# Stacked queries, keys and maxima by transfers instead of turns, the weights' causal corner by GpSimd, 48-row products on 128 rows, and a new order

## What is computed

```python
# block 0: 16 heads of 16 channels
q = split_heads(x @ Wq + bq); k = split_heads(x @ Wk + bk); v = split_heads(x @ Wv + bv)
attn = jnp.einsum('bhqd,bhkd->bhqk', q, k) / jnp.sqrt(jnp.float32(D))
attn = attn + slopes[:, None, None] * (jnp.arange(T) - (T - 1))[None, None, :]
attn = jnp.where(causal, attn, jnp.finfo(jnp.float32).min)
o = jnp.einsum('bhqk,bhkd->bhqd', jax.nn.softmax(attn, axis=-1), v)
out = o.transpose(0, 2, 1, 3).reshape(B, T, C) @ Wo + bo
# block 3: no mask, rope of the halves t1, t2 of each head of q and k
out = jnp.concatenate([t1 * cos - t2 * sin, t1 * sin + t2 * cos], axis=-1)
```

## Time and profile before

| | us |
|---|---|
| three timed runs | 1338.24, 1340.66, 1344.62 |
| median | 1340.66 |
| span of the profiled execution | 1338.5 |
| TensorE matmul busy | 1212.3 (91%) |
| VectorE busy | 938.6 (70%) |
| ScalarE busy | 666.7 (50%) |
| GpSimd busy | 413.8 (31%) |
| bytes moved by transfers | 52.80 MB |

### The profile page before, as it was taken

The page is one execution under the profiler, slowest core; times in us unless marked ns, Lnnn a source line. Parts: engine busy times, 40 slices in busy tenths (PEclk is TensorE's granted clock), DMA queues, the critical chain, the costliest instruction groups (busy, mean ns, idle before and its releaser), DMA issues.

```text
span 1338.5 us, 19778 instructions
## 1 busy us (share of the span) xinstructions
PE 1212.3 (91%) x7788; PEld 796.3 (59%) x7804; DVE 938.6 (70%) x1779; ACT 666.7 (50%) x976; POOL 413.8 (31%) x394
## 2 busy tenths in 40 slices
PE   1789999999999989897789999998999899799988
PEld 0567777677655554554358888886346346445544
DVE  8978575776658999852766645389778676877671
ACT  5335565654767777552133323131772564375473
POOL 3655540034002242402562214034313411421310
PEclk9989999998999999999599999998899889999989
DMA  7200000000060000173530000004101000100200
GB/s 214 67 1 1 2 1 2 2 1 1 1 235 17 16 32 8 56 222 123 132 53 1 24 1 1 1 20 98 29 1 48 1 1 1 47 1 1 95 1 17
DMA packets 31581, 52.80 MB, mean 39 GB/s; under 512 B 5280, under 2 KB 19712, under 8 KB 30720
## 3 DMA queue, kind: packets, MB, share of 16 engines
q1 hardware_dynamic: 27408, 40.57, 9.4%
q0 software_dynamic: 4080, 10.97, 3.7%
HBM read 43.57 MB, written 10.52 MB: 40 GB/s over the span
## 4 chain that ended last, share of the span: by engine, by line
PE 59%; DVE 24%; ACT 6%; issue 5%; POOL 3%; DMA 3%; SPq 0%; DVEq 0%; ACTq 0%; POOLq 0%
PE pair L648 17%; PE bank L648 16%; PE bank L736 7%; PE pair L724 5%; PE pair L704 5%; DVE max L1146 3%; PE pair L686 3%; ACT probs L1641 2%; PE pair L715 2%; DMA gathered<-outbox,slots 2%; POOL gathered L2010 1%; PE pair L694 1%; DVE xn L1065 1%; DVE hidden L1196 1%; PE bank L744 1%
## 5 line engine op out<-in xcount | busy, mean ns | idle before, releaser
L1146 DVE TENSOR_REDUCE max<-pair 128x2 f32<-128x1024 f32 (+3 forms) x256 | 254.7, 1021 | 110.6 <-PE pair L694 57.1
L1641 ACT ACTIVATE probs<-pair 128x1024 f32<-128x1024 f32 (+3 forms) x256 | 212.7, 868 | 94.0 <-PE pair L694 53.5
L704 PE MATMUL pair<-ks,qs 50*128 50x512 f32 (+3 forms) x512 | 117.2, 472 | 17.8 <-DVE max L1146 6.4
L1968 POOL TENSOR_TENSOR h_low<-hidden,h_high 128x512 fp32r<-128x512 f32 x64 | 83.4, 1310 | 133.8 <-ACT h_high L1681 133.4
L736 PE MATMUL bank<-probs,v 128*32 128x512 f32 (+3 forms) x1024 | 114.2, 529 | 0.7 <-ACT probs L1641 0.7
L724 PE MATMUL pair<-qs,ks 52*128 52x512 f32 (+3 forms) x512 | 107.7, 442 | 7.8 <-DVE max L1146 2.7
L704 PEld LDWEIGHTS pair<-ks,qs 50*128 50x128 f32 x512 | 50.9, 198 | 76.3 <-DVE max L1146 28.7
L2028 POOL TENSOR_TENSOR h<-mix_h,h 128x512 bf16<-128x512 f32 x48 | 56.0, 1180 | 125.3 <-DVE mix_h L1537 72.0
L724 PEld LDWEIGHTS pair<-qs,ks 52*128 52x128 f32 x512 | 47.9, 187 | 77.5 <-ACT probs L1641 22.3
L1673 ACT ACTIVATE hidden<-pair 128x512 f32<-128x512 f32 x64 | 37.9, 598 | 89.0 <-PE pair L648 79.6
L1196 DVE SCALAR_TENSOR_TENSOR hidden<-hidden,pair 128x512 f32<-128x512 f32 x64 | 43.6, 682 | 48.7 <-ACT hidden L1673 48.6
(11 more groups left out here) (333 smaller groups left out, 2926.9 us busy)
## 6 DMA issues: line engine op xcount, KB each, us to landing
expert_in<-in_experts_in SPq DMA_DIRECT2D x16, 352.0 KB, 4.7
expert_out<-in_experts_out SPq DMA_DIRECT2D x16, 256.0 KB, 5.8
h<-comb SPq DMA_DIRECT2D x4, 1024.0 KB, 5.2
x<-in_x SPq DMA_DIRECT2D x4, 512.0 KB, 6.1
tern_raw<-in_ffn_in SPq DMA_DIRECT2D x8, 256.0 KB, 5.6
inbox<-zeros SPq DMA_DIRECT2D x4, 512.0 KB, 6.5
tokens<-inbox SPq DMA_DIRECT2D x16, 128.0 KB, 2.5
outbox<-expert_y SPq DMA_DIRECT2D x16, 128.0 KB, 4.0
```

The source lines that it names most:

```text
L704: made = mm(to[:, hh, 0:n], m.qs[g % 2][r0:r0 + AUG + 2, p, qt * P:(qt + 1) * P], m.ks[g % 2][r0:r0 + AUG + 2, p, 0:n], start=True, stop=k ...
L1146: V.tensor_reduce(m.max[:, g % 2, qt, 2 * p:2 * p + 2], to[:, :, 0:n], AX.X, ALU.max).then_inc(*s.done("top"))
L1641: A.activation(m.probs[(2 * kt + p) % 4][:, :, q0:T], to[:, :, q0:T], ACT.Exp, scale=0.25).then_inc(*s.done("exp"))
L1968: Q.tensor_tensor(m.h_low[k][:, j, :], m.hidden[k][j % 2][:, :], m.h_high[k][:, j, :].bitcast(F32), ALU.subtract).then_inc(*s.done("low"))
```

## The change

**Queries and keys.** `qk` makes the products transposed, channels on the partitions and 512 tokens in the columns (weights as the stationary operand), one part for queries and one for keys; `vals` makes the values as before. The number of products and their columns stay. In block 0 ScalarE adds the bias and rounds (`q_high`), VectorE makes the low part (`q_low`). In block 3 ScalarE adds the bias (`biased`), VectorE rotates 128x1024 at a time (`rope`) with tables of cosine and sine, ScalarE rounds, VectorE subtracts. SP's `keep` then writes the parts to DRAM, three transfers of 512 KB each for queries and for keys, at the rows that the stack wants, and GpSimd's `bring` reads each group back as `qs` and `ks`, 512 KB each; there are three of each instead of two. The rows for ALiBi, ones and maxima's ones come once from the inputs (8 transfers of 512 KB from DRAM to DRAM). `cut`, `cut_pool`, `fold`, `folded`, `rope_a`, `rope_b` and `rope_cos` go.

**Maxima.** `shift` negates and splits them, turns 32x32 blocks on VectorE, SP's `max_keep` writes 16 KB to DRAM and GpSimd's `max_bring` reads it into the four rows of the queries' tile. `refold` and `refolded` go.

**Causal corner.** The mask products in `prob` go (those in `score` stay). After `exp`, GpSimd's `causal` sets the weights of later keys to zero in the 128x2x128 corner of each tile, 128 times, and `weigh` waits for it instead of for `exp`. Further rows of the stack, which were zero, hold a large negative number for whole stretches of later keys.

**Rows.** `score` and `prob` contract all 64 rows of a head. The 48-row products of `out` (blocks 1 and 3) and `expert_out` contract 128 rows, of which the last 80 are cleared (`spare_clear`, a memset in `expert_folded`).

**Waits.** Block 1's first weights (`front1`) wait for the probabilities of the last sequence's third group instead of for the last `cut_pool`. A sequence's `keep` waits until the sequence two before it has been brought.

```diff
-        pe.wait_ge(*at("folded", k, b, g, 0))
-        pe.wait_ge(*at("folded", k, b, g, 1))
+        pe.wait_ge(*s.brought(k, b, g))
...
-            made = mm(to[:, hh, 0:n], m.qs[g % 2][r0:r0 + AUG + 2, p, qt * P:(qt + 1) * P], m.ks[g % 2][r0:r0 + AUG + 2, p, 0:n], start=True, stop=k == 3)
+            made = mm(to[:, hh, 0:n], m.qs[k][slot][r0:r0 + STACK, p, qt * P:(qt + 1) * P], m.ks[k][slot][r0:r0 + STACK, p, 0:n], start=True, stop=k == 3)
...
-        pe.wait_ge(*at("refolded", k, b, g))
-        q0 = kt * P if k == 0 else 0
+        pe.wait_ge(*s.max_brought(k, b, g))
+        q0, slot = kt * P if k == 0 else 0, s.slot(b, g)
...
-        if k == 0:
-            made = masked(to[:, :, q0:q0 + P], m.mask_kq)
...
-            pe.wait_ge(*at("exp", k, b, g, kt, p))
+            pe.wait_ge(*(at("causal", b, g, kt, p) if k == 0 else at("exp", k, b, g, kt, p)))
...
-                made = products(to[:, cols], [(m.shared_h[k][0:n_rows, c, tok], m.shared_w[k][0:n_rows, c, :]) for c, n_rows in enumerate((P, I - P))], start=False, stop=k == 1)
+                made = products(to[:, cols], [(m.shared_h[k][:, c, tok], m.shared_w[k][:, c, :]) for c in PAIRS], start=False, stop=k == 1)
...
-        products(to[:, 0:C], [(m.expert_hT[e % 2][0:n_rows, c, :], m.expert_out[e % RING][0:n_rows, c, :]) for c, n_rows in enumerate((P, I - P))]).then_inc(*s.done("expert_out"))
+        products(to[:, 0:C], [(m.expert_hT[e % 2][:, c, :], m.expert_out[e % RING][:, c, :]) for c in PAIRS]).then_inc(*s.done("expert_out"))
...
+        V.transpose(m.max_rows[k][g % 2][:, :].bitcast(F32), m.minus_max[k][g % 2][:, :].bitcast(F32)).then_inc(*s.done("shift"))
...
+    def bring(k, b, g):
+        slot = s.slot(b, g)
+        for i in PAIRS:
+            pool.wait_ge(*s.kept(k, b, i))
+        pool.wait_ge(*s.loaded("extra3" if k == 3 else f"extra{b % 2}"))
+        if G * b + g >= 3:
+            b2, g2 = (b, 0) if g == 3 else (b - 1, g + 1)
+            pool.wait_ge(*s.last("prob", [(k, b2, g2, kt, p) for kt in range(TT) for p in PAIRS]))
...
+        for i, to in enumerate((m.qs[k][slot], m.ks[k][slot])):
+            Q.dma_start(to[:, :, :], kept[k, b % 2, i].rearrange("(g p r) t -> g r p t", g=G, p=2)[g]).then_inc(*s.bringing(b, g))
+
+    def max_bring(k, b, g):
+
+        pool.wait_ge(*s.max_kept(k, b, g))
+        rows = kept_max[k, b, g].rearrange("(n h c) q -> h c n q", h=4, c=2 * TT)
+        Q.dma_start(m.qs[k][s.slot(b, g)][MAX_ROW:P:P // 4, :, :].rearrange("h p (t n q) -> h (p t) n q", t=TT, q=32), rows).then_inc(*s.max_bringing(b, g))
...
+    def causal(b, g, kt, p):
+
+        pool.wait_ge(*at("exp", 0, b, g, kt, p))
+        corner = m.probs[(2 * kt + p) % 4][:, :, kt * P:(kt + 1) * P]
+        Q.affine_select(corner, corner, [[0, 2], [1, P]], ALU.is_ge, 0.0, base=0, channel_multiplier=-1).then_inc(*s.done("causal"))
...
+    def keep(k, b, i):
+
+        sp.wait_ge(*at("q_high", k, b, i))
+        sp.wait_ge(*at("q_low", k, b, i))
+        if b >= 2:
+            for g in range(G):
+                sp.wait_ge(*s.brought(k, b - 2, g))
+        rows = kept[k, b % 2, i].rearrange("(c r j) t -> j r c t" if k == 0 else "(r c j) t -> j r c t", c=KC, j=TERMS)
+        high, low = m.q_high[i], m.q_low[k][i]
+        for j, part in enumerate((high, low, high) if i == 0 else (high, high, low)):
+            send(rows[j], part[:, :, :].bitcast(F32), s.keeping(i))
+
+    def max_keep(k, b, g):
+        sp.wait_ge(*at("shift", k, b, g))
+        send(kept_max[k, b, g], m.max_rows[k][g % 2][:, :].bitcast(F32), s.max_keeping(b, g))
...
+    "bring": "12 13 15 34 65 85 101 119 136 145 157 169 182 197 208 222 336 337 339 351 359 361 360 375 379 380 381 395 398 400 402 405",
+    "max_bring": "23 39 43 83 89 113 131 142 155 163 181 195 206 219 228 239 344 349 355 358 365 374 377 378 387 392 397 399 401 403 409 412",
```

461 lines of the change are left out of this document (249 added, 212 removed), and 284 rows, old and new, of the table DUE.

## The result

The changed kernel takes 1267.57 us (median of 4 runs, 1266.41 to 1273.99) against 1339.45 for the kernel before, a ratio of 0.946 with a 95% interval of 0.943 to 0.950. The prediction said 1271, range 1235 to 1315.

A forecast was written before the change was run, and what follows sets the result against it. TensorE's queue, worked off in fixed order, was taken as the bound: 1338.5 - 99 (work and waits leaving) + 11 + 9 + 6 + 3 (new waits) = 1268.5 us of span, + 2.2 = 1271 us; range 1235 to 1315.

The forecast's parts named there:

- Turns: TensorE, blocks 0 and 3: 96 sets of 8 turns leave, at 0.72 us each, gaining 69 us (60 to 76).
- Masks: TensorE, block 0: 128 sets of four mask products behind the probabilities go, at 0.07 us each, gaining 9 us.
- selects: GpSimd, block 0: 128 causal selects between exp and weigh, 0.5 us each, add 9 us of waits (0 to 35).
- 48 rows: TensorE, out parts and 16 experts: zero-padded products save 0.28 us per four, gaining 13 us (9 to 14).
- The maxima's way: Blocks 0 and 3: maxima through DRAM take 9.3 us a group, partly covered by TensorE work, costing 11 us (6 to 37).
- Start of block 3: Chain from last query or key product to first score takes 25 us against 16.1 of cover, costing 6 us (0 to 15).
- Start of block 0: Same chain without rotation, 20 us, with two feed-forward units ahead of the scores, costing 3 us (-5 to 15).
- All new waits are hidden: Blocks 0 and 3: only 2 or 3 of the 29 us of new waits remain, giving 1244 us; chance 0.14.
- Queued transfers: SP's queue: maxima stand behind the next sequence's keeps, up to 21 us late, adding 36 us, 1307 us; chance 0.09.
- the third rival: GpSimd's transfers wait for VectorE, 2.2 us on each of 32 maxima, 25 us of it showing, 1296 us; chance 0.04.
- The slower rival: GpSimd becomes the bound of block 0 from 1.3 us a select; at 2.0 us, 1349 us; chance 0.07.

The follow-up runs named there:

- the run with the other order: Changed kernel with the first group's eight score parts ahead of the mixture's first two parts on TensorE at block 3's start: 1272.0 us, 0.9488.

## Why the prediction was right

**The bound** was read rightly: TensorE's queue. What leaves it counts for the most part, but not in full: 58 of the turns' 75 us.

**Turns, 69 us.** Put back alone they cost 58 by the timed runs, 59 to 65 by the profiles, and 68 to 75 in TensorE's busy time. The price of a set (0.72) was right for the engine, but only about 0.61 of it is on the path. The term is some 11 us too large, with 5 of uncertainty, since it assumed that what follows is always ready. The turns were put back into the new order, so what they cost in the old one is not measured.

**Masks, 9 us, and selects, 9 us of waits.** Together they were taken for zero; undoing both costs 4.4, with 5 of uncertainty. The waits were 0.7: the work between a probability and its weighing covers a select of 0.41 wholly. So the term for the selects failed. The term for the masks, 9 us at 0.07 a set, took a set at the low end, where the mean is 0.12; what they were worth on the path is not shown by themselves.

**48 rows, 13 us.** 16 measured, 10 to 21, and 9 to 13 by stages. Right, also in its parts: 4.0 in the experts' stretch, 4.0 in block 3.

**The maxima's way, 11 us.** 0.7 measured. The step that failed is the store's price: 4.0 us was read from a store of 128 KB, and 16 KB take 1.4. The trace before had nearer rows, loads of 48 KB by SyncE in the middle of the kernel:

```profile
powers<-in_spline_powers SPq DMA_DIRECT2D x1, 48.0 KB, 1.7
powers<-in_spline_steps SPq DMA_DIRECT2D x1, 48.0 KB, 2.2
```

The lower end of the term (6 us, with a store of 2.5) was still too dear. With 1.4 for the store the same sum over the same list of covers gives a way of 6.7 us, with one group short, by 0.5, which is about what the trace has. The Trainium skill's rule (DMA: Bandwidth & Descriptors, "Anatomy of one DMA — SWDGE (gpsimd) path"), 2.04 us for each of the two, made the way 6.9. The rule is stated for transfers that GpSimd issues, which only the load is: 2.4 here. SyncE's store took 1.4. The measured sum of the two, 3.8, is near the rule's 4.1 because one is above it and the other below, but it was closer than the row that I preferred.

**Start of block 3, 6 us.** 6.8 us of idle time stand there, but for the mixture's weights, not for queries and keys. I had priced the cover at 16 us; from the last key product (864.5) to the first score (901.0) TensorE had 36.5 us, of which it waited 6.8, so the cover was 30. And the chain took 36 and not 25: 14 to the issue of the last store, where bias, rotation and split were put at 7, 6 for that store (10.4 forecast for the stores), and 15 to the landing of the keys at 900.2, where 7.5 was forecast, since the load stood behind the weights on GpSimd's queue. Two errors of over 10 us cancelled. Had the weights come earlier, the keys would have held TensorE nearly as long, as the run with the other order shows. The sign named for this, a first score some 25 us after its last product, did not come true: it was 36.5.

**Start of block 0, 3 us.** The first score starts at 59.9 instead of 72.7, and TensorE has idled 37.4 us by then in both: 0.

**The waits that were not forecast** are the 31 us by which idle time rose: 12.7 in block 0, 10.7 in blocks 1 and 2, 7.7 in block 3, and by cause 13.5 for banks held by maxima and exponentials, 5.9 for the weights, and the rest mostly in block 1. I had forecast 29 us of new waits on transfers and selects and 8 of old ones gone, 21 more idle time; it is 31, nearly all for other causes. TensorE's busy time I had forecast down by 69 + 9 + 13 = 91; it is down by 104. The sum was right because these two misses, 10 and 13 us, nearly cancel, and that is luck. Undone one by one, turns, masks with selects, and short rows cost 58 + 4.4 + 16 = 78 us, with some 9 of uncertainty, where the whole change gained 72; what else changed, the waits and the order, costs about what lies between. The prediction named as a sign a wait of 11 us on the maxima's transfer in 10 to 15 places; there is one, of 0.7. It named TensorE's busy time down by 85 to 95; it is 104.

**The rivals.** "All new waits are hidden" was true of the waits it named and still did not give 1244, because it took every wait for one of them. Queued transfers showed most where the two blocks start, with 13 to 18 us for a load of 5 in block 3 and 7 to 11 in block 0. The maxima's store, which that rival had up to 21 us late, took 1.4 to 4.0 us from issue to landing. GpSimd's load of the maxima took 2.4 in the median (2.3 to 5.5), so the 2.2 us more on each that the third rival took from VectorE are not there either. The slower rival's mechanism is real and begins sooner than I had it.

What stays open: what the new order is worth by itself, and why TensorE waits longer in block 1. Blocks 1 and 2 together still became 5.7 us shorter with 16.4 us less of TensorE's busy time, so it looks like a gain that arrives where VectorE is due anyway, but no run here took it apart.

## What to carry to other kernels

When work leaves the engine that bounds, look for what next frees its banks: in the list of waits before the change the waits on maxima and exponentials were already there, 12.5 and 5.4 us, and after it they were 19.2 and 12.2. Price a small transfer from small transfers at a quiet place of the trace (1.7 and 2.2 us for 48 KB here); the row of a large one put 4.0 where 1.4 stood. GpSimd, which works in order, hurt at 71% busy, well before it was full, and what was asked for behind 2.3 MB on its queue came 9 us late. A run that gives the expected number can still do it in another way: compare the waits and the busy time too.
